# A graph message pass whose list of softmax chunks ends in two chunks of six pairs instead of one of twelve

## The reference

```
h_src = h_all[edge_type, src]
h_dst = h_all[edge_type, dst]
scores = einsum('ehd,hd->eh', h_src, attn_src) + einsum('ehd,hd->eh', h_dst, attn_dst)
scores = where(scores > 0, scores, 0.2 * scores)
amax = maximum(segment_max(scores, dst, num_segments=n), 0.0)
w = exp(scores - amax[dst])
w = w / (segment_sum(w, dst, num_segments=n) + 1e-12)
out = segment_sum(h_src * w[..., None], dst, num_segments=n)
```

## Time and profile before

| | us |
|---|---|
| median of 3 runs (3123.8 to 3129.41) | 3125.5 |
| span of the profiled execution, first to last instruction | 3122.1 |
| median less that span | 3.4 |
| last gather of the message pass issued by POOL | 865.74 |
| last vector instruction of the message pass starts | 913.76 |
| first vector instruction of the next stage starts | 915.37 |

### The profile page before, as it was taken

One profiled execution on the slowest core, in us unless ns is written; L12 is line 12 of the kernel. 1 busy time (PEld: TensorE's weight loads), 2 busy tenths in 40 slices (PEclk: granted clock), 3 DMA queues, 4 the chain that ended last, 5 costly groups with the idle time before them and its releaser, 6 DMA issues. The chain is left out here.

```text
span 3122.1 us, 44085 instructions
## 1 busy us (share of the span) xinstructions
PE 2437.5 (78%) x12032; PEld 1808.1 (58%) x12032; DVE 1410.9 (45%) x3370; ACT 1080.1 (35%) x2815; POOL 1372.3 (44%) x1391
## 2 busy tenths in 40 slices
PE   3899457667669989999994788887655987875996
PEld 3465234444447768888873455554554765654675
DVE  6555356666673200000006211223577665555767
ACT  2422234444432112232222444335302654442320
POOL 1122477777710230000005777777450777775300
PEclk8999777878879899999997899888855999998998
DMA  5256444444410035566544433333293333333001
GB/s 194 91 172 200 139 111 114 118 115 114 113 43 1 34 115 176 178 195 192 177 153 126 139 105 106 106 105 106 72 320 117 100 104 103 102 103 118 30 1 42
DMA packets 241516, 370.86 MB, mean 119 GB/s; under 512 B 65485, under 2 KB 171545, under 8 KB 241308
## 3 DMA queue, kind: packets, MB, share of 16 engines
q0 software_dynamic: 63632, 179.42, 19.6%
q1 hardware_dynamic: 147200, 157.34, 16.0%
q10 hardware_dynamic: 30476, 31.66, 3.0%
HBM read 306.69 MB, written 61.61 MB: 118 GB/s over the span
## 5 line engine op out<-in xcount | busy, mean ns | idle before, releaser
L1135 POOL DMA_INDIRECT ag_rows<-rows,e_bsrc x392 | 390.6, 996 | 244.5 <-SPq L1146 116.4
L1353 POOL DMA_INDIRECT at_rows<-values,e_brow x392 | 389.4, 993 | 139.8 <-issue 92.0
L2563 POOL DMA_INDIRECT cm_rows<-rows,e_bsrc x392 | 371.6, 948 | 140.0 <-issue 92.3
L1429 PE MATMUL at_part<-at_msg,x 128*128 128x265 f32 x880 | 277.7, 461 | 87.9 <-DVE at_msg L1584 51.6
L2643 PE MATMUL cm_part<-cm_rows,cm_one 128*128 x880 | 265.7, 441 | 96.7 <-SPq L2570 78.8
L1160 PE MATMUL banks<-ag_msg,ag_one 128*128 128x258 f32 x880 | 241.6, 410 | 98.5 <-DVE ag_msg L1192 54.6
L2643 PEld LDWEIGHTS cm_part<-cm_rows,cm_one 128*128 128x128 f32 x880 | 173.9, 214 | 181.0 <-issue 160.4
L2084 POOL DMA_INDIRECT je_y<-expert_out,slots x50 | 47.7, 954 | 522.5 <-POOLq L75 507.2
L1429 PEld LDWEIGHTS at_part<-at_msg,x 128*128 128x128 f32 x880 | 184.0, 225 | 158.8 <-DVE at_msg L1584 80.6
L1160 PEld LDWEIGHTS banks<-ag_msg,ag_one 128*128 128x128 f32 x880 | 167.8, 200 | 157.9 <-DVE ag_msg L1192 71.3
L2765 DVE TENSOR_TENSOR h<-h,cm_part 128x256 f32 x220 | 92.2, 419 | 360.2 <-PE cm_part L2643 330.1
(11 more groups left out here) (614 smaller groups left out, 4114.6 us busy)
## 6 DMA issues: line engine op xcount, KB each, us to landing
x_w<-in_L_ffn_W1p SPq DMA_DIRECT2D x32, 1024.0 KB
x_w<-in_L_ffn_W2p SPq DMA_DIRECT2D x32, 1024.0 KB
values<-p_hv ACTq DMA_DIRECT2D x25, 1088.0 KB, 4.9
p_brow<-local_row SPq DMA_DIRECT2D x44, 320.0 KB, 3.8
xn_acc<-local_row SPq DMA_DIRECT2D x44, 320.0 KB, 5.6
xn_acc<-low_row SPq DMA_DIRECT2D x49, 256.0 KB
expert_in<-z_z POOLq DMA_DIRECT2D x8, 1024.0 KB
x_xr<-expert_in SPq DMA_DIRECT2D x32, 256.0 KB, 2.7
```

The source lines that it names most:

```text
L1135: pool.indirect_dma_start(rows[:, b % slots, k, :], None, table, bass.IndirectOffsetOnAxis(index[:, k, b:b + 1], 0)).then_inc(gathered[b % ...
L1353: pool.indirect_dma_start(rows[:, b % RING, k, :], None, table, bass.IndirectOffsetOnAxis(e.block_row[:, k, b:b + 1], 0)).then_inc(gathere ...
L1429: last = pe.matmul(part[:, n % deep, 0:wide], one[:, n // U % 2, k, n % U, :], msg[:, n % 4, k, :], start=(k == 0), stop=(k == K2 - 1))
L2563: pool.indirect_dma_start(rows[:, b % SLOTS, k, :], None, table, bass.IndirectOffsetOnAxis(e.block_src[:, k, b:b + 1], 0)).then_inc(gather ...
```

## The change

Three things. The list of chunks ends in two chunks of six pairs (208 to 213 and 214 to 219; their chains start at n = 202 and n = 208). The score copies of pairs 208 to 219 stand at n = 197 to 208, so that the last copy of a six-pair chunk stands just before its step 0; those of all other pairs stand where they were. And since the last chunk's step 0 falls on the same n as the step 6 of the chunk before, a table holds several steps for one n. Places that found a pair's chunk by dividing by 16 now look it up.

```diff
-CHUNKS = [(lo, min(CH, G - lo)) for lo in range(0, G, CH)]
+END = 6
+LONG = (G - 2 * END) // CH
+assert G == LONG * CH + 2 * END
+CHUNKS = [(lo, CH) for lo in range(0, LONG * CH, CH)] + [(lo, END) for lo in range(LONG * CH, G, END)]
+CHUNK_OF = [(pc, n - lo) for pc, (lo, m) in enumerate(CHUNKS) for n in range(lo, lo + m)]
...
-    step_of = {lo - LEAD + i: (pc, lo, m, i) for pc, (lo, m) in enumerate(CHUNKS) for i in range(LEAD + 1)}
+    steps_at = {}
+    for pc, (lo, m) in enumerate(CHUNKS):
+        for i in range(LEAD + 1):
+            steps_at.setdefault(lo - LEAD + i, []).append((pc, lo, m, i))
+    fetch_at = {}
+    for lo, m in CHUNKS:
+        for j in range(m):
+            fetch_at.setdefault(max(-LEAD, lo + j - FREE, lo - LEAD - (m - 1) + j if m < CH else -LEAD), []).append(lo + j)
...
-            for n in range(FREE - LEAD):
-                fetch(n)
             for n in range(-LEAD, G):
                 if n >= 0 and n % U == 0 and n + U < G:
                     hots(n // U + 1)
-                if n + FREE < G:
-                    fetch(n + FREE)
+                for ahead in fetch_at.get(n, ()):
+                    fetch(ahead)
                 if n > 0 and n % 8 == 0 and n // 8 + 1 < NT:
                     take(n // 8 + 1)
-                if n in step_of:
-                    softmax(*step_of[n])
+                for step in steps_at.get(n, ()):
+                    softmax(*step)
```

More of the change, by code:

```diff
@@ L970, in _ @@
             act.wait_ge(made, 1)
-            full, rest = G // CH, G % CH
-            for at, many, wide in ((0, full, CH), (full, 1, rest)):
+            for at, many, wide in ((0, LONG, CH), (LONG, 2, END)):
                 of = slice(at * CH, at * CH + many * wide)
@@ L1453, in fetch @@
             def fetch(n):
-                pc, j = n // CH, n % CH
+                pc, j = CHUNK_OF[n]
                 if n % U == 0:
@@ L1536, in softmax @@
                     if pc:
-                        dve.tensor_copy(tips[:, now, :, 0:1], tips[:, ago, :, CH:CH + 1])
-                        dve.tensor_copy(inc_h[:, :, 0:1], heads_of(car[:, ago], CH + 1)[:, :, CH:CH + 1]).then_inc(reset, 1)
+                        had = CHUNKS[pc - 1][1]
+                        dve.tensor_copy(tips[:, now, :, 0:1], tips[:, ago, :, had:had + 1])
+                        dve.tensor_copy(inc_h[:, :, 0:1], heads_of(car[:, ago], had + 1)[:, :, had:had + 1]).then_inc(reset, 1)
                     else:
@@ L1590, in add_up @@
                     dve.wait_ge(summed, n)
-                if n % CH == 0:
-                    pc = n // CH
+                if n in first:
+                    pc = first[n]
                     dve.wait_ge(fade_kept, pc + 1)
```

## The result

| | before | changed |
|---|---|---|
| median of 5 runs each, us | 3126.03 (3123.8 to 3129.41) | 3137.9 (3133.43 to 3140.17) |
| ratio, 95% interval | | 1.0034 [1.0023, 1.0045] |
| span of the profiled execution, us | 3122.1 | 3131.6 |

The change makes the kernel 0.34% slower, 7 to 14 us by the interval; the medians are 11.9 us apart. The profiled execution of the changed kernel is the quickest of its five, 3133.43 us.

A forecast was written before the change was run, and what follows sets the result against it. Gathers on POOL pace the pass, but the change acts only in the 44.7 us tail after the last block, bound by a chain of waits. Span 3122.1 + 15.5 = 3137.6, plus 3.4: 3141 us, range 3136 to 3145 (8 in 10: 3131 to 3146).

The forecast's parts named there:

- The late copies: Before the first six-pair chunk's `at_slope`: copies of pairs 211 to 213 behind the matrices delay it 1.7 to 2.5 us, taken 2.0.
- Until the first DVE operation of the new chain: Second chain's start: product of pair 207, scores, `at_slope`, then the maximum at 901.6 to 902.4 us, taken 902.0.
- From there to pair 214: Second chain, from its first DVE operation to the weighing of its first pair, six pairs in between: 15.0 us.
- the 4.7 us: Old last chain: the exponent's delay behind matrices; in the new chain DVE and PE become the bound before it is won.
- The last six pairs: End of the stage after the second chain: six pairs with PE catching up, the fade and last product, 11.2 us.
- its low end: Low end of the forecast's +11 to +19 us: +11.2 us, using 9.3 us for the last six pairs at free pace.
- The sum of 15.5 us: Whole tail: 14.0 us for the second chain, plus 2.0 for late copies, less 0.5 for smaller operations and fewer copies.
- The 3.4 us: Whole kernel: how far the median stands over the profiled span, added to 3137.6 to give 3141 us.
- the chain hides behind the pairs: Rival in the tail: pairs fill the second chain's waits, only DVE's own work is added, 6.3 us, 3131.8; chance 0.08.
- gathers bind: Rival at the first six-pair chunk: step 0 waits for blocks, so it starts sooner; near +2 us, 3127; chance 0.04.
- ACT set free from n = 186: Rival on ACT, n = 186 to 192: no holding behind copies, chunk before sooner, at most 2.11 us; gain chance 0.02.
- a clock that stays up: Second chain on PE: pair products save 1.0 us each, sum near 10.5 us; within the low-end rival, chance 0.10.

The follow-up runs named there:

- The two kernels with moved matrices: Against the kernel before: ACT's one-hot matrices put behind the softmax steps of the same n, ratio 0.9974; or moved behind further steps too, 0.9981.
- the spread steps: Against the kernel before: the last chain's steps stand at n = 198 to 208 instead of 202 to 208, ten pairs between them instead of six; ratio 0.9988.
- the kernel with both edits: Against the kernel before: last chain's steps spread over n = 198 to 208, and one-hot matrices behind the softmax steps of the same n; ratio 0.9973.

## Why the prediction was right

Its direction, its sum and its reason held: the second chain comes after the last gather and little covers it. Term by term, counted from the weighing of pair 192:

- *The late copies*, 2.0 us for `at_slope`: from pair 192 to pair 202 it took 882.61 - 862.37 = 20.2 us against 882.36 - 863.91 = 18.5 before, 1.8 us more, the same in the kernel that has only this edit (1042.9 - 1022.6 = 20.3). What it is worth at the end was measured as 1.2 us in the one list and 2.7 to 3.7 in the other (1.7, and 1.3 to 2.2, counted from pair 186).
- *Until the first DVE operation of the new chain*: 901.43 - 862.37 = 39.1 us after pair 192, where the terms gave 902.0 - 863.91 + 2.0 - 0.5 = 39.6.
- *From there to pair 214*: 915.64 - 901.43 = 14.2 us for the 15.0. The exponent waited 0.8 us for the matrices (ready at 911.51, started at 912.33), but `at_w` then 2.06 us for PE. That is what the prediction had: other work becomes the bound before the 4.7 us are won. The two kernels with moved matrices show it too, though they won 4 to 5 us over two chains.
- *The last six pairs*: 926.72 - 915.64 = 11.1 us for the 11.2. The 9.30 us that the prediction gives for a free pace, and uses for its low end, cover seven pairs, 213 to 219; six take 914.19 - 905.85 = 8.3, by the row below, so the low end was 1 us too high. Nothing hung on it.

```profile
905.85 0.70 DVE L1584 TENSOR_TENSOR at_msg<-at_rows,at_w 128x528 f32<-128x528 f32 x1
```

The sum of 15.5 us came out as 14.1 in one profile and 15.0 in the other. (The 3.4 us that the prediction adds for what lies around the span are only in part that: in the changed kernel's runs it is 1.8 us, as 3133.43 against 3131.6, and the rest is that the profiled execution before was quicker than the median. As medians are compared on both sides, the forecast is not changed by it.) The median moved by 11.9 us, and 14.1 is at the edge of its interval; what lies between was not traced to a cause, and the time outside the tail differed by 4.6 us between the two profiles, though no edit touches it. How much of the 14.1 us is the chain's length and how much the lower clock, 0.69 for the 0.91 of before from 896 to 914.2 us, the runs don't part; the prediction had put the clock into its terms by taking them from the old chain as it ran.

The rivals: that the chain hides behind the pairs is refuted at this place, and the spread steps show what it takes, namely pairs between the steps. That gathers bind is refuted: the last block was announced at 868.3 us, 10 us ahead of the three late copies at 878.64, and on the slower chips, where it was announced 3 us ahead of pair 192, the tail grew by 15.0 us. ACT set free from n = 186 shows nothing: from pair 186 to 192 it took 14.7 us for 14.8. The clock stayed low until 924 us, longer than the 918 that the prediction named: 0.68, 0.69 and 0.62. The case of a clock that stays up did not come. The rule of the Trainium skill that activity releases the clock ("TensorE: Matmul & The Clock Gate", What's actually happening) agrees with these rows; no run here tested it.

What the prediction had not seen is that the place of ACT's matrices relative to the last copy can cost 5 us by itself, more than the 2.0 it gave the late copies. In the changed kernel matrices stand directly ahead of the last three copies of the first new chunk, and nothing of the kind stands directly ahead of the last copy of the second.

## What to carry to other kernels

Find first where the engine that sets the pace stops. A dependency chain that costs next to nothing ahead of that point can cost nearly its length behind it (about 12 us here), so there one wants fewer chains, and pairs of work between their steps, rather than shorter chunks that may begin sooner. On an engine that works in order, look at what stands between the last input of a chain and its first step: a block of work that waits for another engine can be added to the chain with its wait.

## What the runs showed of the hardware

Between the maximum of the chain of pair 208 and that pair's weighing, the granted clock was 1.00 in the kernel with both edits and 0.91 with the spread steps alone (1032.2 to 1050.4 us). Where six pairs lie between the steps it was 0.55 before (880.5 to 896.2), 0.63 with the matrices moved (1040.36 to 1054.35) and 0.62 in the changed kernel, there with the scores of the second chain. So it was higher in both kernels with spread steps; why is not shown, since PE was busy for about the same share of the time in the kernel with both edits and in the changed one, 11.53 of 17.00 us and 15.66 of 22.60. A pair's products take 2.13 us at the lower level and 1.13 at the higher, so part of the 9.3 us may be the clock; how much, the runs don't part.

The same program took 3126 us on one chip and 3624 to 3632 on the others, with the same 0.94 us for the shortest gather instruction on POOL. In the changed kernel, 150 of the 516 us between the two spans lie between the first and the last gather of this message pass: 392 gathers were issued over 507.5 us (356.7 to 864.2) on the one and 657.1 us (357.0 to 1014.1) on the other. POOL waited 26.2 us for SP's signal of a free place in the first and 151.5 us in the second, while from the last gather's issue to the last block's signal it took 4.1 and 4.0 us. A slower landing is thus not shown. From the weighing of pair 192 to the end it took 64.4 and 65.3 us.
